# A fused MoE-convolution, linear-attention and BitLinear kernel: convolution and attention outputs held channel by token instead of token by channel

## The reference

```
x = x + conv(groupnorm(x))         4 experts, two 96x96 1x1 convolutions each, relu between them,
                                   mixed by coefficients of the two best gates
t = tokens(x)
t = t + attn(layernorm_tokens(t))  q, k, v; k and v through where(t >= 0, t + 1, exp(t)); k^T v per
                                   head, a fixed mask, q times it, a projection
t = t + bitlinear2(gelu(bitlinear1(layernorm_tokens(t))))   sign weights; outputs scaled by the
                                   largest magnitude of a group of 6 images and clipped
```

## Time and profile before

| | |
|---|---|
| median of 3 executions | 851.54 us (850.2 to 852.54) |
| the profiled execution, its time | 856.85 us |
| the profiled execution, its span | 855.0 us |
| PE busy in the span | 809.4 us (95%) |
| DVE busy | 632.5 us (74%) |
| ACT busy | 461.7 us (54%) |
| POOL busy | 181.0 us (21%) |
| the pipeline over the images | about 66 to 660 us |

### The profile page before, as it was taken

The page is one execution under the profiler, slowest core; times in us unless marked ns, Lnnn a source line. Parts: engine busy times, 40 slices in busy tenths (PEclk is TensorE's granted clock), DMA queues, the critical chain, the costliest instruction groups (busy, mean ns, idle before and its releaser), DMA issues.

```text
span 855.0 us, 17997 instructions
## 1 busy us (share of the span) xinstructions
PE 809.4 (95%) x6053; PEld 624.7 (73%) x6053; DVE 632.5 (74%) x1977; ACT 461.7 (54%) x654; POOL 181.0 (21%) x216
## 2 busy tenths in 40 slices
PE   6888999999999999999999999999999799999991
PEld 3456688888888888888888888888888655555550
DVE  3585477777776777777677777777777257999997
ACT  2453354454454445445444544544443299988981
POOL 1460222223223222322322232232232000000000
PEclk8899899999999999999999999999999599999997
DMA  9950001111000001100000110000010010563433
GB/s 214 213 118 16 15 30 30 30 29 56 28 28 28 28 28 33 52 28 28 28 28 28 41 43 28 28 28 28 28 42 14 15 43 0 150 196 105 142 113 113
DMA packets 19979, 48.69 MB, mean 57 GB/s; under 512 B 4561, under 2 KB 4847, under 8 KB 19951
## 3 DMA queue, kind: packets, MB, share of 16 engines
q1 hardware_dynamic: 19552, 47.72, 20.1%
q10 hardware_dynamic: 399, 0.60, 0.2%
HBM read 29.51 MB, written 18.67 MB: 56 GB/s over the span
## 4 chain that ended last, share of the span: by engine, by line
PE 86%; DVE 4%; SPq 3%; ACT 3%; issue 2%; POOL 1%; DMA 1%; DVEq 0%; ACTq 0%; POOLq 0%
PE slot L1007 18%; PE slot L988 11%; PE slot L856 10%; PE slot L1053 9%; PE slot L1017 6%; PE slot L1014 6%; PE slot L1172 5%; PE slot L1143 5%; PE slot L1204 4%; PE slot L1208 4%; PE slot L1002 3%; SPq L443 2%; DMA big<-in_x 1%; PE slot L920 1%; ACT big L822 1%
## 5 line engine op out<-in xcount | busy, mean ns | idle before, releaser
L1007 PE MATMUL slot<-w2s,hT 128*112 128x96 f32 x1344 | 162.7, 269 | 0.0
L1421 DVE TENSOR_SCALAR xh<-t,ln_mv,ln_rs 112x96 f32<-112x96 f32 x434 | 109.2, 323 | 60.0 <-POOL ln_rs L605 60.0
L1007 PEld LDWEIGHTS slot<-w2s,hT 128*112 128x112 f32 x1344 | 141.6, 177 | 10.7
L748 ACT ACTIVATE hT<-slot,b1c,w_unit 128x784 f32<-128x784 f32 x96 | 95.9, 1004 | 90.8 <-PE slot L988 90.8
L755 ACT ACTIVATE stage<-slot,minus_one 112x768 f32<-112x768 f32 x64 | 52.5, 821 | 119.0 <-PE slot L1053 118.9
L579 POOL TENSOR_TENSOR xn_lo<-xn,xn_hi 96x784 f16<-96x784 f32 x32 | 53.4, 1669 | 245.0 <-ACT xn_hi L737 245.0
L605 POOL TENSOR_TENSOR ln_rs<-ln_ve,pow_half 112x7 f32<-112x7 f32 x62 | 91.8, 1481 | 4.8
L1014 PE MATMUL slot<-big,W1b 99*128 (+1 forms) x360 | 90.5, 332 | 0.1
L1017 PE MATMUL slot<-big,W1b 96*128 (+1 forms) x360 | 90.2, 332 | 0.0
L1427 DVE TENSOR_REDUCE ymax<-slot 128x784 f32 (+1 forms) x90 | 83.9, 960 | 6.4 <-PE slot L1017 5.9
L1053 PE MATMUL slot<-qkvw,xh1T 97*112 97x192 f32 x448 | 86.4, 335 | 0.9 <-ACT xh1T L769 0.9
(11 more groups left out here) (194 smaller groups left out, 1363.4 us busy)
## 6 DMA issues: line engine op xcount, KB each, us to landing
out<-t2T SPq DMA_DIRECT2D x56, 294.0 KB, 3.1
xs<-in_x SPq DMA_DIRECT2D x32, 294.0 KB, 3.1
big<-in_x SPq DMA_DIRECT2D x7, 1176.0 KB, 15.8
xs<-out SPq DMA_DIRECT2D x24, 294.0 KB, 3.3
big<-out SPq DMA_DIRECT2D x1, 1764.0 KB, 11.2
out<-big SPq DMA_DIRECT2D x6, 294.0 KB, 2.6
big<-in_x SPq DMA_DIRECT2D x2, 588.0 KB, 25.0
con<-shape_consts ACTq DMA_DIRECT2D x1, 445.5 KB, 6.3
```

Source lines behind the costliest of these rows:

```text
L748: nc.scalar.activation(hT[:, t, :].rearrange("p (a n) -> p a n", a=2), halves((0, one, 2)[t], P), ACT.Relu, scale=w1_unit[:, t:t + 1], bia ...
L1007: ins = mm(o[:, j, :], hT[:, t, j * TOK:(j + 1) * TOK], w2s[:, v, t, :], start=False, stop=t == TILES - 1, skip_group_check=True)
L1421: ins = V.tensor_scalar(dst[:, j, :], src[:, j, :], ln_mv[n][:, j, 0:1], ln_rs[n][:, j:j + 1], ALU.subtract, ALU.mult)
```

## The change

What it does, by engine. PE: `mix` takes a 128x96 block of `w2s` as stationary and the hidden tile's 2 x 392 tokens as moving operand; x and the bias are no longer added in PSUM. The three tiles go one after the other into slot 1, all of them ahead of `kv`. The attention output has `R` as stationary operand and 2 x 392 tokens as moving. The results, `t1cm` and `t2T`, are channels, and `to_tokens` transposes each of them so that DVE can normalize tokens. The transposes of x and of t2 go. DVE: one instruction adds mixing result, bias and x into `t1cm`; the sum t2 is written straight into `t2T`; normalization happens in place in `tok1` and `tok2`. `stats` and `apply` of the second layer norm move from the end of a step into the next step. ACT: two copies from PSUM to `tok1` and `tok2` in place of the one to `t2T`; the group norm of the next image goes between the two exponentials. POOL: the second layer norm's rstd goes first. SP: x is reloaded when `t1_ready` says so; the store follows `t2_ready`. The slots no longer alternate. The bias is prepared as a column (`bias2`) by two small DVE instructions, which replaces the splitting of b2 into bfloat16 parts on POOL and its two scalings on DVE; two parameter loads fewer. The remainder step at the end goes.

TensorE:

```diff
-            def mix(v, k, r, with_x, j0, n):
-                o = chunks(k, CHUNKS, P, C)
-                if with_x:
-                    for j in range(j0, j0 + n):
-                        tr(o[:, j, :], xs[r][:, j * TOK:(j + 1) * TOK], start=j % CH_A == 0)
-                mm(o[:, j0:j0 + n, :], ones_b[0:B_ROWS, :],
-                   bias2_parts[:, v:v + 1, :].to_broadcast([B_ROWS, n, C]),
-                   start=v == 0, stop=False, skip_group_check=True)
-                for j in range(j0, j0 + n):
-                    for t in range(TILES):
-                        ins = mm(o[:, j, :], hT[:, t, j * TOK:(j + 1) * TOK], w2s[:, v, t, :],
-                                 start=False, stop=t == TILES - 1, skip_group_check=True)
+            def to_tokens(k, src, done):
+                for j in range(CHUNKS):
+                    ins = tr(flat(k)[0:TOK, j * P:j * P + C], src[:, j * TOK:(j + 1) * TOK], start=j % CH_A == 0)
+                ins.then_inc(done, 1)
+
+            def mix(v, k, t):
+                for h in range(2):
+                    ins = mm(S[k][0:C, h, 0:HALF], w2s[:, v, t, :], hT[:, t, h * HALF:(h + 1) * HALF],
+                             start=t == 0, stop=t == TILES - 1, skip_group_check=True)
                 return ins
...
                     hidden(0, 0, r)
+                    pe.wait_ge(tok1_ready, i)
                     wait_count(pe, ymax_done, 3 * (i - 3) + 2)
-                    hidden(1, one, r)
+                    hidden(1, 1, r)
+                if ffn:
+                    pe.wait_ge(t2_ready, i - 1)
+                    to_tokens(3, t2T[r], tok2_in_psum)
+                if experts and not first:
                     wait_count(pe, ymax_done, 3 * (i - 3) + 3)
                     hidden(2, 2, r)
...
-                    to_channels(0, xh1, x1T_ready)
+                    to_channels(0, tok1, x1T_ready)
...
                 if experts:
-                    pe.wait_ge(h_ready, 3 * i + 2)
-                if out_:
-                    pe.wait_ge(t2_ready, i - 1)
-                    to_channels(one, t2, t2p_ready)
-                if experts:
-                    pe.wait_ge(h_ready, 3 * i + 3)
-                    mix(1, 2, r, not first, 0, 2)
+                    if not first:
+                        pe.wait_ge(h_ready, 3 * i + 2)
+                    mix(1, 1, 0)
+                    mix(1, 1, 1)
+                    if not first:
+                        pe.wait_ge(h_ready, 3 * i + 3)
+                    mix(1, 1, 2).then_inc(y_mixed, 1)
...
                 if attend:
                     pe.wait_ge(xh1T_ready, i)
-                    wait_count(pe, t2_ready, i - 1)
-                    kv(0, other, 0, CH_A)
-                if experts and not second:
-                    mix(1, 2, r, not first, 2, CH_A - 2).then_inc(yx_part, 1)
+                    if ffn:
+                        pe.wait_ge(tok2_ready, i - 1)
+                    elif not second:
+                        pe.wait_ge(t2_ready, i - 1)
+                    kv(0, 3, 0, CH_A)
...
                 if attend:
                     kv(1, 0, CH_A, CHUNKS - CH_A)
                 if scales:
                     y1_max_row()
+                if ffn:
+                    pe.wait_ge(xh2_ready, i - 1)
+                    to_channels(2, tok2, x2p_ready)
                 if experts:
-                    mix(1, 2, r, not first, CH_A, 1)
-                if out_ and ffn:
-                    pe.wait_ge(xh2_ready, i - 1)
-                    pe.wait_ge(f_ready, 2 * i - 1)
-                    to_channels(other, xh2, x2p_ready)
...
+                    pe.wait_ge(t1_ready, i + 1)
+                    to_tokens(1, t1cm[r], tok1_in_psum)
...
-                if out_ and ffn:
-                    pe.wait_ge(t1_ready, i + 1)
-                    ffn_tile(i - 2, 1, 2).then_inc(y_ready, 1)
+                if ffn:
+                    pe.wait_ge(tok1_ready, i + 1)
+                    ffn_tile(i - 2, 1, 1).then_inc(y_ready, 1)
...
-                    for j in range(CHUNKS):
-                        ins = mm(flat(one)[0:TOK, j * P:j * P + C], xh1T[:, j * TOK:(j + 1) * TOK], R[:, :],
+                    for h in range(2):
+                        ins = mm(S[3][0:C, h, 0:HALF], R[:, :], xh1T[:, h * HALF:(h + 1) * HALF],
                                  start=True, stop=True, skip_group_check=True)
```

DVE, the order of a step after the change (general branch left out), then ACT and SP:

```diff
+                if ffn:
+                    dve.wait_ge(tok2_ready, f + 1)
+                    stats(1, tok2, 2 * i - 1)
+                if attend:
+                    feature_map(0, 3, 0, CH_A)
+                if ffn:
+                    apply(1, tok2, tok2, f, xh2_ready)
...
+                    with dve.Else():
+                        dve.wait_ge(y_mixed, i + 1)
+                        V.scalar_tensor_tensor(t1cm[r][:, :].rearrange("p (a n) -> p a n", a=2), halves(1, C),
+                                               bias2[:, 1:2], xs[r][:, :].rearrange("p (a n) -> p a n", a=2),
+                                               ALU.add, ALU.add).then_inc(t1_ready, 1)
+                if attend:
+                    feature_map(1, 0, CH_A, CHUNKS - CH_A)
+                if ffn:
                     dve.wait_ge(hi_ready, f + 1)
...
+                    mask_a(i, 3)
...
+                    dve.wait_ge(tok1_ready, i + 1)
+                    stats(0, tok1, 1 if isinstance(i, int) and i == 0 else 2 * i)
+                if ffn:
+                    for t in range(TILES):
+                        absmax(f, t, t)
                 if attend:
                     dve.wait_ge(ao_ready, i)
-                    V.tensor_tensor(t2[:, :, :], t1[1 - r][:, :, :], chunks(one, CHUNKS, P, C),
+                    wait_count(dve, t2T_stored[1 - r], 16 * (m + r - 1))
+                    V.tensor_tensor(t2T[1 - r][:, :].rearrange("p (a n) -> p a n", a=2), halves(3, C),
+                                    t1cm[1 - r][:, :].rearrange("p (a n) -> p a n", a=2),
                                     ALU.add).then_inc(t2_ready, 1)
+                if experts:
+                    apply(0, tok1, tok1, i, xh1_ready)
```

```diff
                     relu(1, 1)
+                if ffn:
+                    act.wait_ge(tok2_in_psum, i - 1)
+                    tokens(tok2, 3, tok2_ready)
+                if experts and not between:
                     relu(2, 2)
...
-                if out_:
-                    act.wait_ge(t2p_ready, i - 1)
-                    wait_count(act, t2T_stored[r], 16 * (m - 1))
-                    nc.scalar.copy(*channels(t2T[r][:, :], one)).then_inc(t2T_evac, 1)
-                if attend:
-                    exp_kv(0, other, 0, CH_A)
-                    exp_kv(1, 0, CH_A, CHUNKS - CH_A)
...
+                    exp_kv(0, 3, 0, CH_A)
                 if experts and next_:
                     norm_image(m + r, 1 - r, i + 1)
+                if attend:
+                    exp_kv(1, 0, CH_A, CHUNKS - CH_A)
...
+                if experts:
+                    act.wait_ge(tok1_in_psum, i + 1)
+                    tokens(tok1, 1, tok1_ready)
```

```diff
+            def load_next(m, r):
+                sp.wait_ge(t1_ready, 2 * m + r + 1)
+                sp.dma_start(xs[r][:, :], x_bcn[2 * m + r + 2]).then_inc(xs_loaded[r], 16)
...
+                sp.wait_ge(t2_ready, i)
+                sp.dma_start(out_bcn[i - 1], t2T[1 - r][:, :]).then_inc(t2T_stored[1 - r], 16)
```

More of the change, by code:

```diff
@@ L244, in build @@
         xn_lo = [sb(f"xn_lo{r}", [C, HW], F16) for r in range(2)]
[L245 to L247 removed]
+        tmp = stage[0:C, 5376:5376 + HW]
+        t1cm = [sb(f"t1cm{r}", [C, HW]) for r in range(2)]
         ln_st = sb("ln_st", [TOK, CHUNKS, 6])
@@ L251, in build @@
         ln_rs = [sb(f"ln_rs{n}", [TOK, CHUNKS]) for n in range(2)]
-        xh1 = sb("xh1", [TOK, CHUNKS, C])
-        xh2 = sb("xh2", [TOK, CHUNKS, C])
+        w0_image = sb("w0_image", [TOK, CHUNKS])
+        tok1 = sb("tok1", [TOK, CHUNKS, C])
+        tok2 = sb("tok2", [TOK, CHUNKS, C])
         xh1T = sb("xh1T", [C + 1, HW])
@@ L609, in step @@
                 i = 2 * m + r
+                if not isinstance(i, int) or i >= 2:
+                    rstd(1, i - 2)
                 if next_:
@@ L741, in channels, with tokens, step @@
                         flat(k)[0:C, 0:CHUNKS * P].rearrange("p (j t) -> p j t", t=P)[:, :, 0:TOK])
-            def step(m, r, experts=True, attend=True, out_=True, ffn=True, next_=True, between=False):
+            def tokens(dst, k, done):
+                nc.scalar.copy(dst[:, :, :], chunks(k, CHUNKS, P, C)).then_inc(done, 1)
+            def step(m, r, experts=True, attend=True, ffn=True, next_=True, between=False):
                 i = 2 * m + r
-                one, other = one_other(r)
                 def relu(t, n):
@@ L839, in _ @@
             gelu_tile(0, 0, 0)
-            step(LAST // 2, 1, experts=False, attend=False, ffn=False)
             ffn(0, 0, started=True)
@@ L1043, in y1_max_spread, with step @@
```

(12 more changed lines are left out.)

209 lines of the change are left out of this document (84 added, 125 removed).

## The result

The changed kernel takes 1012.74 us (median of 4 executions, 1008.63 to 1013.86) against 851.19 us before: a ratio of 1.189, 95% interval 1.185 to 1.193. Slower was forecast, 956 us in a range up to 1005; the loss is 162 us where 104 was expected.

What follows compares the result with a forecast made beforehand. PE was taken to bound the loop. Thirty images at -1.67 us work and +3.0 gap (+40), 20 clock falls of 3.1 (+62) and 3 for tight covers, on 851.5, gave 956 us; range 888 to 1005.

Steps and rivals of the forecast that it cites:

- TensorE's work: PE per image: mixing 6.25 to 4.62 us, attention output 1.36 to 1.32, together -1.67, leaving 17.02.
- the new wait: PE before the transposes of tok2, behind exponential, feature map and normalization: chain 3.81 us, 0.99 covered, gap 2.82.
- The rule of the Trainium skill on idle gaps: Warns only of longer idle gaps on TensorE; by it the clock holds, about 893 us; as a rival, chance 0.2.
- the rivals' ways: Clock holds, 892 us (0.2); longer falls, 1020 (0.1); shorter wait, faster, 801 with no gap (0.06); no change (0.03).
- Rival 2: Clock falls behind the gap last twice 6.7 us in 20 images: 1020 us, chance 0.1.
- the normalization takes 1.77: Last link on DVE in the chain before the transposes of tok2: 1.77 us, as in the old profile.
- DVE is then normalizing anyway: ACT's group norm of the next image holds the second exponential for two us, costed at nothing.
- sign named ahead: Expected in the changed profile, such as images above 20 us and 2.8 us idle before the transposes of tok2, thirty times.
- The clock: PE's clock falls to half speed for 6.7 us after the gap: 3.1 us each in 20 of 30 images, +62 us.
- The gap: PE's idle time per image after keys and values: 2.82 us plus 0.2 waiting for t1cm, 3.0 in all.

Runs made afterwards that it cites:

- e4: Changed kernel with the first part of keys and values moved behind the first mixing tile, the other two tiles after it; 906.03 us, ratio 1.056.
- e7: Changed kernel, VectorE normalizing tok2 and adding t1cm before the first feature map, ScalarE's group norm before the first exponential, POOL's subtraction after the normalization; 825.92 us.
- e10: Changed kernel with only VectorE's order of e7 (normalization and t1cm ahead of the first feature map), ScalarE and POOL unchanged; 918.96 us, ratio 1.076.
- e1: Changed kernel with POOL's subtraction for the next image waiting until VectorE has normalized tok2; 958.23 us, ratio 1.121.
- e8: e1 with 10 dummy matmuls on TensorE in the remaining gap before the transposes of tok2; 909.36 us, ratio 1.062.
- e5: Kernel before the change, with all pieces of its mixing in a row ahead of keys and values, layouts kept; 978.81 us, ratio 1.147.

## Why the prediction was wrong

**What held.** TensorE's work: mixing 3.95 and attention output 1.32 were as computed. The place of the new wait, its cause and its frequency: e4, e7 and e10 show that the cover ahead of `kv` and VectorE's order behind it make the gap. Its size without POOL: from start to start it is 2.85 us in e1 against 2.82 (2.69 of it shows as idle time). The rule of the Trainium skill on idle gaps (TensorE: Matmul & The Clock Gate, "HAM oscillation"), by which the clock would have held, was rightly set aside: it fell after the 2.7 us of e1 and even the 1.55 us of e4. The changed kernel's own 4.2 us is of the length that the rule warns of, and is no test of it. None of the rivals' ways was taken. Rival 2's 1020 us is nearer to the measured time than the forecast, but by chance: it came from falls of 13.4 us in 20 images, and the trace shows 6.8 us in all of them.

**The step that failed** is in the part on the new wait: "the normalization takes 1.77". It takes 3.26, and the gap is 4.2 and not 2.8. The prediction did see the group norm of the next image move ahead of the second exponential, and costed it at nothing on ScalarE, because "DVE is then normalizing anyway". It did not follow what the move releases: the group norm feeds POOL's subtraction, which before ran at 416.09, beside no normalization, and now starts a microsecond into one. VectorE's instruction does not get on beside POOL's, so one of the seven waits for the rest of POOL's 1.66 us. Nearly every sign named ahead came (images above 20 us, twelve records in a row, the wait on the normalization, PE under 90%, PEclk of 7 to 9); only the length of the idle time told this kernel from the one forecast.

With POOL out of the way (e1) the measured 958.2 us stands beside the 956 forecast, and the changed kernel is 54 us above that: 30 times 1.5 of gap is 45, the rest a dearer fall. That e1 comes so close is partly luck. The forecast had 20 falls of 3.1 us; e1 has one in every image, at about 2.4 (22.14 less 20.54 in e8, and 0.8 of short waits uncovered there).

**The clock** was the second term, and mis-sized: 20 falls of 3.1 us, 2.1 us per image on average. In the changed kernel it fell in each image of the loop. Filling the gap saves 1.85 us an image (23.89 to 22.04) and uncovers 0.8 us of short waits, so a fall costs about 2.65 us: cheaper than 3.1, but thirty times, 80 us instead of 62.

**Per image**, from start to start: 18.63 before. TensorE's work about -1.75, for e7's 17.69 holds some 0.8 of waits, and 16.9 is left; -1.67 was forecast, so this term was right; the short waits themselves, of which the one before the first BitLinear tile was not foreseen, are hidden under the slow clock in the changed kernel. The gap +4.35 (`kv` could end at 401.34, the transposes start at 405.69), against 3.0. The clock +2.65, against 2.1. That is 23.9, and 30 x 5.26 is 158 of the 162 us.

**What the change could give.** With two moves in other engines' programs and one wait, the same layouts take 825.9 us, 3.5% less than before; the gain of TensorE's work was real, and it was lost behind it.

## What to carry to other kernels

When a saturated engine's order is changed, look at what each waiting instruction of the next engine has in front of it in its queue: work that was ready all along stood behind a feature map that was not. When an instruction moves, follow it through to the engine it feeds; here VectorE's instruction stood still until POOL's had ended, so the new neighbour matters even if both engines have time to spare. And price an idle gap on TensorE with the slow clock behind it; filling it with dummy matmuls is a cheap way to measure that share, and here a gain.

## What the runs showed of the hardware that was not expected

- A VectorE `tensor_scalar` on SBUF (322 ns) that met POOL's `tensor_tensor` (1.66 us) took 1821 to 1839 ns, in every image; POOL's instruction kept its length. A VectorE `scalar_tensor_tensor` with one operand in PSUM ran beside the same POOL instruction in its usual 1.02 us.
- The clock fell after idle times of 1.55 us (e4, every image) and after 1.0 and 0.6 us close together (e5, about half of the images), though 1.7 us had passed without a fall in the kernel before.
- A busy PE is not enough to bring it back: in e5 it stayed at 1.2 GHz for 13.7 us with PE busy for 13.61, most of it in 16-bit matmuls of 392 columns. What distinguishes that stretch from the 3.4 to 6.8 us of the new layout was not isolated.
- Each of the two records of a float32 matmul with 392 moving columns takes 0.33 us (twelve in 3.95), twice the 0.17 of a 16-bit one (`hidden`, eighteen in 2.99): the two records tell only half of what float32 costs.
